# First stage of a ViT tower kernel: in units 8 to 15, five heads of eight of the second factor on GpSimd and three on VectorE

## The reference

```python
dtA = A * dt[:, None]                      # 128 heads x 64 modes
Cc = Bc[None, :, :] * Cc                   # C is the input x: 16 x 128 x 64, complex
Cc = Cc * (jnp.exp(dtA) - 1.0) / A
V = jnp.exp(dtA[:, :, None] * ell)         # ell = 0 .. 1023
K = 2.0 * jnp.einsum('chn,hnl->chl', Cc, V).real
h = K; h = h + attention(layernorm(h)); h = h + ffn(layernorm(h))
```

## Time and profile before

| | us |
|---|---|
| median of 3 runs (1872.11 to 1877.5) | 1872.27 |
| the profiled execution | 1872.55 |
| its span, first to last instruction | 1870.7 |
| TensorE, busy | 1776.9 (95%) |
| VectorE, busy | 1312.0 (70%) |
| ScalarE, busy | 743.5 (40%) |
| GpSimd, busy | 980.0 (52%) |

### The profile page before, as it was taken

One profiled execution on the slowest core, in us unless ns is written; L12 is line 12 of the kernel. 1 busy time (PEld: TensorE's weight loads), 2 busy tenths in 40 slices (PEclk: granted clock), 3 DMA queues, 4 the chain that ended last, 5 costly groups with the idle time before them and its releaser, 6 DMA issues.

```text
span 1870.7 us, 31749 instructions
## 1 busy us (share of the span) xinstructions
PE 1776.9 (95%) x12772; PEld 967.9 (52%) x12772; DVE 1312.0 (70%) x1782; ACT 743.5 (40%) x1085; POOL 980.0 (52%) x692
## 2 busy tenths in 40 slices
PE   0887999999999999999999999999999999999998
PEld 0886656666666656545554344444444444444444
DVE  8995787777788888846656866775665555377775
ACT  6693334333343444322114644444444443122221
POOL 6970334343343343522361576665668776468672
PEclk9998999999999999999999999999999999999999
DMA  2233011110122221254532343433546553634431
GB/s 100 59 90 96 10 60 20 60 42 16 49 81 64 74 66 58 74 179 153 171 108 68 102 128 109 125 112 113 169 147 210 155 168 94 229 106 147 170 117 68
DMA packets 102707, 194.94 MB, mean 104 GB/s; under 512 B 14305, under 2 KB 75489, under 8 KB 92065
## 3 DMA queue, kind: packets, MB, share of 16 engines
q1 hardware_dynamic: 102560, 192.90, 32.2%
HBM read 135.72 MB, written 56.11 MB: 103 GB/s over the span
## 4 chain that ended last, share of the span: by engine, by line
PE 76%; DVE 9%; POOL 2%; issue 2%; ACT 2%; DMA 0%; DVEq 0%; ACTq 0%
PE acc L1611 13%; PE acc L1613 13%; PE acc L1779 9%; PE acc L1744 4%; PE ps_p L1403 4%; PE ps_p L1405 4%; PE ps_p L1404 4%; PE acc L1517 3%; PE ps_t L1430 3%; PE acc L1518 3%; PE acc L1519 3%; PE ps_p L1419 2%; PE ps_p L1421 2%; PE ps_p L1420 2%; PE ps_l L1620 2%
## 5 line engine op out<-in xcount | busy, mean ns | idle before, releaser
L1257 POOL TENSOR_TENSOR prob<-prob,mx 128x1024 f32<-128x1024 f32 x64 | 121.4, 1898 | 361.7 <-DVE mx L2208 361.7
L1403 PE MATMUL ps_p<-x_hi,w_qk 128*128 128x512 f16 x512 | 194.7, 380 | 0.0
L1404 PE MATMUL ps_p<-x_lo,w_qk 128*128 128x512 f16 x512 | 194.0, 379 | 0.0
L1405 PE MATMUL ps_p<-x_hi,w_qk 128*128 128x512 f16 x512 | 194.0, 379 | 0.0
L1310 POOL TENSOR_TENSOR hidden<-up,hidden 128x512 f16<-128x512 f32 x80 | 91.1, 1159 | 141.9 <-ACT hidden L2037 141.5
L1262 POOL TENSOR_TENSOR prob<-prob,sm 128x1024 f32<-128x1024 f32 x64 | 120.2, 1897 | 52.9 <-DVE sm L2215 52.9
L1419 PE MATMUL ps_p<-w_v,x_hi 128*128 128x256 f16 x512 | 140.4, 274 | 3.4 <-PEq L955 2.7
L1871 ACT ACTIVATE pth<-ps_t 128x512 f16<-128x512 f32 x128 | 76.1, 595 | 163.8 <-PE ps_t L1430 163.8
L1420 PE MATMUL ps_p<-w_v,x_hi 128*128 128x256 f16 x512 | 140.4, 274 | 0.0
L1421 PE MATMUL ps_p<-w_v,x_lo 128*128 128x256 f16 x512 | 140.4, 274 | 0.0
L2460 DVE SCALAR_TENSOR_TENSOR up<-acc,gu_scale,up 128x512 f32<-128x512 f32 x120 | 90.0, 750 | 61.5 <-PE acc L1613 61.0
(11 more groups left out here) (403 smaller groups left out, 4550.5 us busy)
## 6 DMA issues: line engine op xcount, KB each, us to landing
q_raw<-in_gu_q SPq DMA_DIRECT2D x42, 1024.0 KB, 6.2
hid_parts<-hidden_parts SPq DMA_DIRECT2D x16, 1376.0 KB, 7.1
hidden_parts<-hidden SPq DMA_DIRECT2D x42, 512.0 KB, 3.5
down_raw<-in_down_q SPq DMA_DIRECT2D x22, 512.0 KB, 3.6
w_raw<-in_w_qk SPq DMA_DIRECT2D x8, 1024.0 KB, 4.8
h_tokens<-n_tok SPq DMA_DIRECT2D x16, 512.0 KB, 3.8
o_parts<-ot SPq DMA_DIRECT2D x32, 256.0 KB, 2.3
wv_raw<-in_w_o SPq DMA_DIRECT2D x8, 1024.0 KB, 4.8
```

Of the source, the lines that this page charges most:

```text
L1257: nc.gpsimd.tensor_tensor(prob[s % 2][p][:], prob[s % 2][p][:], bc(mx[p][:], H, 2), ALU.subtract).then_inc(s_sub[p], 1)
L1403: nc.tensor.matmul(out[:], w[:, j % 2, m, 0, at], xn_hi[:, k, tok], start=(k == 0), stop=False)
L1404: nc.tensor.matmul(out[:], w[:, j % 2, m, 0, at], xn_lo[:, k, tok], start=False, stop=False)
L1405: last = nc.tensor.matmul(out[:], w[:, j % 2, m, 1, at], xn_hi[:, k, tok], start=False, stop=(k == KT - 1))
```

## The change

`CUT` becomes two constants, 3 for units 0 to 7 and 5 for units 8 to 15. In the later units GpSimd's L284 makes five heads (640 elements) and VectorE's L554 three (384 elements); the copy of `a2` into PSUM (L547) shrinks from 40 to 24 elements. No instruction, semaphore or wait is added or removed, and none changes its place.

```diff
--- before.py
+++ after.py
@@ -76,7 +76,7 @@
 
 UH = 8
 UNITS = H // UH
-CUT = 3
+CUT_EARLY, CUT_LATE = 3, 5
 TI, TJ = 8, 16
 TAB = 2 * TI + TJ
 STEPS_OF = [P * k for k in range(TI)] + [TJ * k for k in range(TI)] + list(range(TJ))
@@ -170,6 +170,9 @@
 
             return 1 + u * UH // LEAD_H if u < UNITS // 2 else HALF_H // LEAD_H + 1
 
+        def cut_of(u):
+            return CUT_EARLY if u < UNITS // 2 else CUT_LATE
+
         def leads(g):
             return slice(g * LEAD_H, (g + 1) * LEAD_H)
 
@@ -272,7 +275,8 @@
                     tt(a2[:, hs, :], a2[:, hs, :], at[:, hs, :], ALU.subtract).then_inc(s_a2, 1)
 
             for u in range(UNITS):
-                s, ch, cut = u % 2, channels(u), channels(u, 0, CUT)
+                s, ch, share = u % 2, channels(u), cut_of(u)
+                cut = channels(u, 0, share)
                 pool.wait_ge(s_tab, 2 if u < UNITS // 2 else 5)
                 if u >= 2:
                     pool.wait_ge(s_mm, 2 * (u - 1))
@@ -281,7 +285,7 @@
                 pool.wait_ge(s_a1, ready(u))
                 nc.gpsimd.tensor_tensor(four(w[s][0], C), bc(a1[:, ch, :], C, 3), bc(cre[:, ch, :], KT, 2), ALU.mult)
                 pool.wait_ge(s_a2, ready(u))
-                nc.gpsimd.tensor_tensor(four(w[s][1], C)[:, 0:CUT], bc(a2[:, cut, :], C, 3), bc(cim[:, cut, :], KT, 2),
+                nc.gpsimd.tensor_tensor(four(w[s][1], C)[:, 0:share], bc(a2[:, cut, :], C, 3), bc(cim[:, cut, :], KT, 2),
                                         ALU.mult).then_inc(s_wp, 1)
                 if u in (1, 3, 5):
                     for part in range(3):
@@ -538,20 +542,22 @@
 
             def slices(u):
 
-                s, ch, hs = u % 2, channels(u), channels(u, CUT, UH)
+                s, ch, share = u % 2, channels(u), cut_of(u)
+                hs = channels(u, share, UH)
                 dve.wait_ge(s_a2, ready(u))
                 if u >= 2:
                     dve.wait_ge(s_v, 2 * (u - 1))
                     dve.wait_ge(s_wd, u - 1)
                 ts(cuts[:, s, 0:UH, :], tab2[:, ch, TI:2 * TI], 1.0, None, ALU.mult).then_inc(s_cut, 1)
-                ts(cuts[:, s, UH + CUT:2 * UH, :], a2[:, hs, :], 1.0, None, ALU.mult).then_inc(s_cut, 1)
+                ts(cuts[:, s, UH + share:2 * UH, :], a2[:, hs, :], 1.0, None, ALU.mult).then_inc(s_cut, 1)
 
             def second_factor(u):
-                s, hs = u % 2, channels(u, CUT, UH)
+                s, share = u % 2, cut_of(u)
+                hs = channels(u, share, UH)
                 dve.wait_ge(s_cut, 2 * (u + 1))
                 if u >= 2:
                     dve.wait_ge(s_mm, 2 * (u - 1))
-                tt(four(w[s][1], C)[:, CUT:UH], bc(cuts[:, s, UH + CUT:2 * UH, :], C, 3), bc(cim[:, hs, :], KT, 2),
+                tt(four(w[s][1], C)[:, share:UH], bc(cuts[:, s, UH + share:2 * UH, :], C, 3), bc(cim[:, hs, :], KT, 2),
                    ALU.mult).then_inc(s_wd, 1)
 
             def second_power(u, part):
```

## The result

The changed kernel takes 1876.14 us (median of 21 runs), the kernel before 1872.34 (21 runs); the ratio is 1.0023, with a 95% interval from 1.0017 to 1.0030, so 3.2 to 5.6 us slower. The profiled execution takes 1875.03 us with a span of 1873.2, 2.5 more than the earlier trace rows. The forecast was 1873.9, within 1871.5 to 1877.2: the direction was right, and the size of 1.6 us too small, for the medians lie 3.8 us apart. A few executions take far longer (2 of these 21, at 2690 and 3800 us, and the profiled one of e4_both_before); the ratios leave them out, and no length is read from them.

What follows compares the result with a forecast made beforehand. No engine was taken as the bound by itself; L284 governs iterations where it holds L584. 0 (L554) + 1.55 (lock) = 1.6 us, on a median of 1872.27, gave 1873.9 us, range 1871.5 to 1877.2.

Steps and rivals of the forecast that it cites:

- VectorE's saving costed at nothing: L554 gets 0.26 us shorter, but ScalarE ends last before L581, so idle time grows from 0.30 to 0.56: 0 us.
- Rival C: VectorE, not ScalarE, is last before L581, so the shorter L554 pays: down to -2.1 us, 1870.2; chance 0.07.
- GpSimd's own time costed at nothing: L284 grows 0.44 us to 1.28, taken up by GpSimd's next wait for a TensorE product: none on the path.
- The lock, L(k) = L(k-2) + 12.62: Where GpSimd's L284 holds VectorE's L584, the end of L593 comes 12.62 us after that two iterations earlier, not 12.18.
- read at least one operand from PSUM or have a single one, and show no such stretching: Claim that in VectorE's round only L584 is stretched by GpSimd, so other instructions there were given no added cost.
- The walk: Iterations 7 to 14 stepped through, requests for L584 timed from the preceding L593 or ScalarE's chain: L(14) 1.55 us later.
- 1.55 us pass to the end: After product 15 one chain runs through tokens, norm and features to the barrier, passing on the full 1.55 us.
- rival A: At iteration 13 L584 is caught behind L284, and the next waits behind conversion L301: 4.4 us, 1876.7; chance 0.2.
- D: As rival A, but the second L301 is granted ahead of L584: 7.2 us, 1879.5; chance 0.03.
- Rival B: L584 of iteration 12, asked for 0.2 us sooner, passes between L282 and L284: 0.7 us, 1873.0; chance 0.13.
- the tie at iteration 13: L584 asked for at 132.60 as L282 ends at 132.63; taken as served ahead of L284, L(13) 0.8 us later.

Runs made afterwards that it cites:

- e4_both_before: The kernel before, with the small VectorE instructions L584, L783 and L790 rewritten so none has two SBUF tensor inputs, L790 as two one-column instructions; 1871.85 us, ratio 0.9994.
- e5: The changed kernel with GpSimd kept to three heads in units 8 to 15, heads 3 and 4 left out of the output; 1871.99 us, ratio 1.0000.
- e4b: The kernel of e4_both_before run once more, for a profile; 1871.18 us, ratio to the kernel before 0.9994.
- e3: The changed kernel with L590 and L789 each given one tensor and pointer scalars, and L796 split into two one-column instructions; 1872.03 us, ratio to before 1.0001.
- e2: The changed kernel with L789 given one tensor and pointer scalars and L796 split into two one-column instructions, L590 unaltered; 1874.05 us, ratio to before 1.0011.
- e10: The changed kernel unaltered, run again for a second profile; 1875.10 us, ratio to the kernel before 1.0014.
- e7: The kernel of e3 with one head of eight on GpSimd and seven on VectorE in units 8 to 15; 1871.98 us, ratio to before 0.9995.

## Why the prediction was right, and where its size was wrong

- *VectorE's saving costed at nothing: right.* L554 from 0.82 to 0.55 us (forecast 0.56), idle time from 0.30 to 0.56 (forecast 0.56), e5 42.56 against 42.58 us. Rival C, faster, is excluded by it; e4b and e3 exclude it with the lock gone too.
- *GpSimd's own time costed at nothing: right up to iteration 14.* L288 takes 1.27 us (forecast 1.28), and e3 with that length is as short as e4b without it. For the end the prediction looked at the conversion's reader alone. L595 stands behind the conversion too once the rounds are short (1.42 us in e3, 0.96 in e4b); in the changed kernel it came after the conversion and took 0.81.
- *The lock, L(k) = L(k-2) + 12.62: right.* The changed kernel's iterations 8 to 10 end 6.24, 12.60 and 18.85 us after iteration 7, forecast 6.27, 12.62 and 18.89. Taken alone, in e2, it costs 1.49 us up to iteration 14, forecast 1.55, and L590's total over iterations 8 to 14 rises from 2.15 to 3.93 us, forecast about 2 more. In the changed kernel it rises to 2.68 only. (The 128.12 that the prediction gives for k = 12 should be 128.10, as in the trace.)
- *The sentence that the other VectorE instructions "read at least one operand from PSUM or have a single one, and show no such stretching": wrong, and this is the step that failed.* L783 has two tensors in SBUF, `wv_big` and `b_top`, and L790, two columns with a pointer scalar, stretched to 0.46 us in the trace I had. I had looked only for L584. The walk used 4.36 us from L593 of iteration 10 to the next L584, and 4.82 from that of iteration 13, as if these were fixed; inside the first lay the 0.22 us of an L783 that had just caught a gap, inside the second the 0.46 of L790. A shift of 0.25 us against GpSimd was enough to miss the gap. The two holds, 1.76 and 1.95 us, are 3.1 us more than the freed forms take in e2. Of that 2.2 us arrive at iteration 14 (46.29 against 44.07), for the most part since L590 then takes 0.16, 0.16, 0.63 and 0.16 us in iterations 11 to 14, 1.2 us less in all than in e2: in 11 and 12 GpSimd has finished L288 when it is asked for, and in 14 the conversion is under way, which does not hold it. So the cost is 1.49 us for L590 as forecast, and 2.2 us for two holds that the sum did not have.
- *The end of the stage, "1.55 us pass to the end": right as to the chain, but not as to its clock.* In both profiles of the changed kernel 0.88 us were given back, as the features of unit 14 were turned in 1.07 instead of 1.94 us.
- *Rivals.* The time of rival A was near the measured one (1876.7), but its mechanism did not occur, and both profiles of the changed kernel speak against it: L590 was asked for in the middle of the first half of the conversion (141.69, within 140.34 to 143.18) and took 0.16 us. Rivals A and D had priced that wait at up to 2.5 and 5.4 us. The rule that the prediction cites, of a GpSimd instruction that reads SBUF, agrees with the rows of L286 and L288 and not with those of L305. Rival B did not occur; the tie at iteration 13 was never reached in the changed kernel.
- *The range: luck.* 1876.14 lies within it only because its upper end was taken from rival A. By the same rule it would have ended without A about 0.5 us above the forecast, at 1874.4, and the two holds that made the difference were in none of the cases.
- *What stays open.* Why the conversion holds L595 and not L590 is open. The profiles account for 2.5 us of span, 2.41 of them at the last L599 (161.53 against 159.12). The medians of 21 runs lie 3.8 us apart, those of the later comparison 2.7 (e10, ratio 1.0004 to 1.0024). In an execution where unit 14's features fall to the half clock the stage would be 3.7 us longer instead of 2.8, by my estimate from the 1.07 and 1.94 us; that some executions do so is argued and not shown, as only two executions of the changed kernel have a trace, both at the full clock.

## What to carry to other kernels

Before giving GpSimd more of a shared job, list every VectorE instruction beside it that has two SBUF tensors, however small, and every tensor_scalar from SBUF to SBUF of two columns or more, and see in the trace where each is asked for and when GpSimd's instruction then under way ends: the price of a small one is the rest of that instruction, and it jumps when the order of the two flips. Look which GpSimd instructions hold which of them: here the tensor_tensor ones held L590 and the tensor_scalar did not. A product of two 128 x 1 columns can be freed for 0.05 us (0.21 instead of 0.16), as a tensor with a pointer scalar. Time taken from an engine counts only where the next thing on its queue isn't waiting for another engine; find that idle time first, and move work into it rather than away from it.

## What the runs showed of the hardware

- A VectorE instruction with two tensors in SBUF was held by GpSimd's tensor_tensor instructions and not by its tensor_scalar ones, in two places. One is L590 beside L305, above. The other is near the start of the kernel: in the trace of before, L492 (tensor_tensor of 128x128, both inputs in SBUF) begins at 26.08 and takes 0.37 us while GpSimd's tensor_scalar L219 runs from 25.78 to 26.75.
- L796, a tensor_scalar of 128x2 with one tensor and a pointer, is held like one with two tensors (1.95 us beside L286), while the same in two instructions of 128x1 takes 0.33 us for both in e2, and L590 of 128x1 with a pointer 0.21 us beside L288 in e3. L595, 128x1024 with pointers, SBUF to SBUF, is held too (1.43 us beside the conversion, 0.81 alone). The Trainium skill, "SBUF — State Buffer", section "SBUF: two separate sides", names instructions "in a 2-port perf mode" beside those with two SBUF inputs as users of the shared port pair. That would fit 2 and 1024 columns being held and 1 column free; no run here changed the mode alone.
- The full clock of TensorE (granted 1.00) outlasted 3.50 us of idleness in both profiles of the changed kernel, and 3.47 us of it ended at half clock (0.50) in the kernel before; e2 and e4b, also after 3.47 us, lie between (1.37 and 1.30 us for eight transposes), and e7 took 1.80 us after 3.51. The length of the idle time alone doesn't decide it.
